# Quantising w_fc in transposed layout, 32-column chunk patterns and one more step of lag in an attention and block-quantised FFN kernel

## The reference, cut to what matters

```python
x = x + attn(layernorm(x));  x = x + ffn(layernorm(x))
# attention: 128 chunk summaries per sequence, each the mean of 64 normalised rows
q = x @ Wq + bq;  k = summary @ Wk + bk;  v = summary @ Wv + bv       # 16 heads of 64
out = softmax(mask(q k^T / 8)) @ v @ Wo + bo
# ffn, 1024 -> 4096 -> 1024
h = gelu(quant(x) @ quant(w_fc).T + b_fc);  y = quant(h) @ quant(w_proj).T + b_proj
def quant(v):   # blocks of 32 along the last dimension
    scale = exp2(floor(log2(max(|block|))) - 3);  return round(v / scale) * scale
```

## Time and profile before

| | us |
|---|---|
| median of three runs | 1062.04 |
| the profiled execution, whole | 1060.65 |
| its span on the slowest core (core 3) | 1059.1 |
| spans of the other cores | 1043.5 to 1057.7 |
| PE, DVE, ACT busy in the span | 759.1, 695.3, 390.2 |

### The profile page before, as it was taken

The page is one execution under the profiler, slowest core; times in us unless marked ns, Lnnn a source line. Parts: engine busy times, 40 slices in busy tenths (PEclk is TensorE's granted clock), DMA queues, the critical chain, the costliest instruction groups (busy, mean ns, idle before and its releaser), DMA issues.

```text
span 1059.1 us, 13616 instructions; the slowest of 8 cores (1043.5 to 1059.1 us)
## 1 busy us (share of the span) xinstructions
PE 759.1 (72%) x4554; PEld 427.1 (40%) x4554; DVE 695.3 (66%) x1039; ACT 390.2 (37%) x623; POOL 114.9 (11%) x171
## 2 busy tenths in 40 slices
PE   0304433635585647769769699999999999999973
PEld 0102111212233212224226475766667675858431
DVE  3557537776733576967557699796969696877601
ACT  2335426565641454425443342323323141505000
POOL 2201213121201000001100000000000000000011
PEclk9997766766877656779889889999999999999987
DMA  8999997899718874743275611232313141302023
GB/s 219 219 198 171 214 232 168 225 212 205 181 66 147 198 199 124 241 146 113 106 219 197 236 34 41 41 60 27 75 20 80 20 81 19 63 6 36 1 40 41
DMA packets 87877, 130.33 MB, mean 123 GB/s; under 512 B 54008, under 2 KB 54144, under 8 KB 85760
## 3 DMA queue, kind: packets, MB, share of 16 engines
q0 software_dynamic: 23312, 57.95, 27.2%
q1 hardware_dynamic: 64496, 71.51, 25.8%
HBM read 112.93 MB, written 25.17 MB: 130 GB/s over the span
## 4 chain that ended last, share of the span: by engine, by line
PE 53%; DMA 16%; DVE 14%; issue 7%; ACT 5%; SPq 3%; DVEq 0%; ACTq 0%; POOL 0%; POOLq 0%
PE psY L1029 11%; PE psX L1029 10%; DMA wst<-wpj_in 6%; PE psS L979 6%; PE psV L979 5%; PE psT L979 4%; PE psO L979 4%; DMA xs<-xoth 4%; SPq L146 3%; DMA wst<-wfc_in 3%; PE psY L614 3%; DMA sel<-sel_in 2%; DVE uq L394 2%; PE psO L792 2%; PE psT L792 2%
## 5 line engine op out<-in xcount | busy, mean ns | idle before, releaser
L1029 PE MATMUL psY<-wpT,hq 128*128 128x512 bf16 x512 | 154.2, 383 | 6.0 <-DVE ob L1044 6.0
L1029 PE MATMUL psX<-wpT,hq 128*128 128x512 bf16 x512 | 153.9, 382 | 0.6 <-DVE ob L1044 0.6
L481 PE MATMUL psX<-lnb,pats 128*128 128x512 bf16 x32 | 15.8, 594 | 171.6 <-ACT lnb L589 171.6
L990 DVE TENSOR_REDUCE hpart<-h 128x256 f32<-128x1024 f32 x56 | 107.6, 1922 | 13.2 <-ACT h L983 13.2
L983 ACT ACTIVATE h<-psV,bfc 128x256 f32<-128x256 f32 x72 | 34.1, 474 | 208.2 <-PE psV L979 205.0
L979 PE MATMUL psS<-xqT,wfcT 128*128 128x256 bf16 x576 | 77.6, 279 | 8.8 <-ACT h L983 8.8
L979 PE MATMUL psV<-xqT,wfcT 128*128 128x256 bf16 x576 | 77.2, 279 | 9.0 <-DMA xqT<-xq 4.7
L614 PE MATMUL psY<-lnT,WA 128*128 128x512 bf16 x256 | 72.5, 444 | 14.4 <-ACT lnT L316 14.4
L361 ACT ACTIVATE uq<-wst 128x2048 bf16<-128x2048 bf16 x32 | 60.9, 1902 | 55.0 <-DMA wst<-wpj_in 36.0
L1012 DVE TENSOR_TENSOR hq<-h,hM 128x1024 bf16<-128x1024 f32 x64 | 78.1, 1220 | 1.0 <-DVE hM L1003 0.2
L1029 PEld LDWEIGHTS psY<-wpT,hq 128*128 128x128 bf16 x512 | 50.4, 98 | 67.9 <-issue 8.6
(11 more groups left out here) (123 smaller groups left out, 1216.6 us busy)
## 6 DMA issues: line engine op xcount, KB each, us to landing
xr<-xown POOLq DMA_DIRECT2D x32, 512.0 KB, 7.1
wst<-wfc_in SPq DMA_DIRECT2D x16, 1024.0 KB, 7.9
wst<-wpj_in SPq DMA_DIRECT2D x16, 1024.0 KB, 8.9
xs<-xoth POOLq DMA_DIRECT2D x24, 512.0 KB, 11.4
wpq_scr<-uq SPq DMA_DIRECT2D x16, 512.0 KB, 7.8
y<-xr POOLq DMA_DIRECT2D x16, 512.0 KB, 3.2
xt<-y SPq DMA_DIRECT2D x16, 512.0 KB, 3.7
wpT<-wpq_scr SPq DMA_DIRECT2D x16, 512.0 KB, 10.1
```

The costliest lines, as they stand in the source:

```text
L990: tr_ = op("vector", lambda E, c=c, dst=dst: E.tensor_reduce(out=dst, in_=h[:, 4 * c:4 * c + 4, :].rearrange("p e t -> p t e"), axis=AXX, ...
L1029: tk = op("tensor", lambda E, e=e, e4=e4, u=u, hf=hf, a=a: E.matmul(f2[a].rearrange("p (c n) -> p c n", n=64), hq[r][:, e4, 128 * u:128 * ...
```

## The change

The changed kernel does the following.

- w_fc arrives from the host already transposed and tiled, [2048, 2048], so that a job's tile has features on partitions and hidden units in the free dimension. It is quantised in place in `wfcT`. The 16 DMA transposes are gone. Since a block of 32 now crosses partitions, three halvings on DVE reduce within a partition (the last writes 256 numbers a partition), 64 KB go to DRAM (`wmx_d`) and come back as `gat`, [128, 4, 256], the same 32 rows copied to four groups of partitions (256 KB). Two more halvings (512 and 256 wide) end the maximum.
- A job now yields 5 times. Its rounding (`weight_round`) is put one job behind its maxima (`weight_max`). `wst` has 3 buffers, and loads are issued three jobs ahead. The stream gives 4 yields a step, attention 1 after each of scores, o_unit and mix.
- Patterns are 32 columns wide, one slot's chunks, with a second pattern for the six tiles that cross into the next slot. One load of 0.57 MB takes the place of four of 0.5 MB. The summary matmuls write 32 partitions of `psX`.
- The stream has one more step of lag: statistics at step k, 1/std and patterns at k+1, matmuls at k+2. There are 4 `xs` buffers and 3 `lnb`. Own tiles go with steps 0 to 15. Drains of queries come one place later in ACT's list. Wq is loaded at the end of step 1, Wv when the last query is done, which is now inside the stream. Three small tables are loaded at the start.
- Values are computed ahead of the row maxima.
- In `o_unit` the residual add on DVE also gives the sum of the row. Two bn_stats (L803) and a bn_aggr (L807) for each tile go, and a Square with accumulation on ACT (`squares`) takes their place, one small DVE operation before it. `squares` is called after `mix`, and in FC1 of the first group right after each `o_unit`.

```diff
@@ weights @@
-        for i in range(8):
-            jobs += [("fc", i), ("pj", i)]
-        jobs += [("pj", i) for i in range(8, 12)]
+        for i in range(4):
+            jobs += [("fc", i), ("pj", 2 * i), ("pj", 2 * i + 1)]
+        for i in range(4, 8):
+            jobs += [("fc", i), ("pj", 4 + i)]
...
+            t = op("vector", lambda E: E.tensor_tensor(
+                out=u[:, 512:768].rearrange("p (g c) -> p g c", g=2), in0=u3[:, :, 0:128],
+                in1=u3[:, :, 128:256], op=ALU.max), after=[t])
...
+            t = dma("sync", f"gw{g}", wmx_d[i].rearrange("p (c n) -> c p n", c=4), u[:, 512:768], after=[t])
+            yield
+            job[n, "max"] = dma("sync", f"gat{g}", gat[g].rearrange("p c n -> p (c n)"),
+                                wmx_d[i].unsqueeze(0).broadcast_to([4, 32, 1024]),
+                                after=[t, gat_free[g]] + (st["gat"] if g == 3 else []))
@@ weight_round @@
+                t = tree(gat[g].rearrange("p (z c) n -> p z (c n)", z=1), 512, t)
+                t = tree(gat[g].rearrange("p (z c) n -> p z (c n)", z=1), 256, t)
...
-            if n + 2 < len(jobs):
-                load_job(n + 2)
+            if n + 3 < len(jobs):
+                load_job(n + 3)
...
-                t = Q.dma_turn(f"uq{b}", wfcT[:, 2 * i:2 * i + 2].rearrange("p t j c -> p (t j) c"), uq[b],
-                               after=[t] + late)
@@ the generator @@
+            for n in range(len(jobs)):
...
+                yield from weight_max(n)
+                if n + 1 < len(jobs) and eligible(n + 1):
+                    weight_abs(n + 1)
+                if due is not None:
+                    yield from weight_round(due)
+                due = n
@@ the stream @@
-        for k in range(NSTEP + 1):
-            if k >= 1:
+        for k in range(NSTEP + 2):
+            if 1 <= k <= NSTEP:
                 rstd(k - 1)
-                scale_patterns(k - 1)
             if k < NSTEP:
                 other_stats(k)
...
+            background(1 if k < NSTEP else 0)
+            queries()
+            if 1 <= k <= NSTEP:
+                rstd_exp(k - 1)
+                scale_patterns(k - 1)
+            if k - 2 in own_tile:
+                pend = own_mm(k - 2)
+            background(1 if k < NSTEP else 0)
...
             if k - 1 in own_tile:
-                pend = own_apply(k - 1)
-            background(3)
-            queries(1)
-            if k >= 1:
-                add_others(k - 1)
+                own_apply(k - 1)
+            if k >= 2:
+                add_others(k - 2)
                 if k + 2 < NSTEP:
                     load_other(k + 2)
+            background(2 if k < NSTEP else 0)
...
+            if k > 17 and not q_todo and t_wv is None:
+                t_wv = dma("gpsimd", "WA", WA, wv_in.rearrange("(j p) n -> p j n", p=128), after=lnT_free)
@@ o_unit @@
-            ts = op("vector", lambda E: E.bn_stats(out=bn2[:, 6 * hf:6 * hf + 6], in_=xx),
-                    after=[tx, bn2_free["tok"]])
@@ squares @@
+                tq = op("scalar", lambda E, t=t, k=k: E.activation(
+                    out=junk2[t // 8], in_=xr[k], func=ACT.Square, bias=nm2[:, t:t + 1], accum_out=ssq[:, t:t + 1]),
+                    after=[ta, sq_prev["tok"], sel_free[0] if t > 7 else None] + xr_free[2])
```

More of the change, by code:

```diff
@@ L358, in weight_abs @@
         def weight_abs(n):
[L359 removed]
+            kind, i = jobs[n]
+            k, t = wload[n]
             hi = wst[k].bitcast(BF16)[:, 1::2]
[L361 to L380 removed]
+            if kind == "fc":
+                u = wfcT[:, 2 * i:2 * i + 2].rearrange("p t j c -> p (t j c)")
+                free = st["stream_end"] if i >= 8 else []
+            else:
+                b = n_pj["i"] % 2
+                n_pj["i"] += 1
+                u, free = uq[b], uq_free[b]
+                job[n, "b"] = b
@@ new lines, in weight_round @@
+        def weight_round(n):
+            kind, i = jobs[n]
+            u = job[n, "u"]
+            t = job[n, "max"]
+            k = wload[n][0]
+            mm = trm[n % 2]
+            if kind == "fc":
+                g = job[n, "g"]
+                G, E8, Bk = 2, 8, 128
+                pw = gat[g][:, 0]
+                t = tree(gat[g].rearrange("p (z c) n -> p z (c n)", z=1), 512, t)
+                t = tree(gat[g].rearrange("p (z c) n -> p z (c n)", z=1), 256, t)
+            else:
+                G, E8, Bk = 1, 32, 64
+                pw = u[:, 0:64]
+                mm = mm[:, 0:64]
@@ L412, in weights @@
         def weights():
-            for n, (kind, i) in enumerate(jobs):
-                while kind == "fc" and i >= 8 and not st["stream_end"]:
-                    yield
-                yield from weight_job(n)
+            weight_abs(0)
+            due = None
+            for n in range(len(jobs)):
+                if (n, "abs") not in job:
+                    if due is not None:
+                        yield from weight_round(due)
+                        due = None
+                    while not eligible(n):
+                        yield
+                    weight_abs(n)
+                yield from weight_max(n)
+                if n + 1 < len(jobs) and eligible(n + 1):
+                    weight_abs(n + 1)
+                if due is not None:
+                    yield from weight_round(due)
+                due = n
@@ L686, in build_nc @@
         t_k = kv_tok[1]
+        tv = None
+        for half in range(2):
+            for j in range(8):
+                op("tensor", lambda E, j=j, half=half: E.matmul(
+                    psX[:, 512 * half:512 * half + 512], summT[:, j, :], WA[:, j, 512 * half:512 * half + 512],
+                    start=(j == 0), stop=False), after=[t_wv, t_smT, t_sm], sig=False)
+            tv = op("tensor", lambda E, half=half: E.matmul(
+                psX[:, 512 * half:512 * half + 512], orow, brow[:, 512 * half:512 * half + 512],
+                start=False, stop=True), after=[t_bv, t_ones])
+        t_v = op("scalar", lambda E: E.activation(out=vv, in_=psX, func=ACT.Identity), after=[tv])
+        t_wa = tv
+        t_bo = dma("gpsimd", "brow", brow, bo_in, after=[tv])
         t_wo = dma("gpsimd", "WB", WB, wo_in.rearrange("(j p) n -> p j n", p=128), after=[tk])
-        background(4)
+        background(2)
         def load_sel(s):
```

399 lines of the change are left out of this document (213 added, 186 removed).

## The result

Over 20 runs of each on the same chips the changed kernel takes 1068.53 us in the median and the kernel before 1062.12. The ratio of after to before is 1.0057 (95% interval 1.004 to 1.0073). The forecast was 994, the range 955 to 1045, and slower had 0.06. It was wrong in sign and by 75 us.

The account below looks back on a forecast made before the run. PE bounds FFN and attention's slots 2 and 3; DMA throughput or latency the stream. Stream -42, turn -11, attention -20, FC1 +5 make -68 from 1059.1, 991.1; adjusted from span to median, 994 us, range 955 to 1045.

Parts of the forecast that it names:

- The gather itself has five yields: Weight jobs in the stream: store and gather, 2 x 5 us, fit in 13 us, so DVE would not wait.
- rival 4: Stream: DVE waits for store and gather, 32 us where 13 are given; +152 us, 1146 us in all; chance 0.05.
- The milder form: Stream: DVE waits less for store and gather, ending between 1146 and the forecast 994; no time or chance of its own.
- SP's wait for the store: SP's queue: wait for the 64 KB store to land before issuing the gather, 5 us, bounds 3 and 9.6.
- The opening: Stream before step 6: fewer bytes and less blocking by transposes bring step 6's start from 96.5 to 86 us.
- The steps: Stream steps 6 to 21: bounded at once by DMA and PE, both near 9.5 us; 10.4 us a step.
- The end of the stream: From the last statistics to the last summary matmul: 8 us, with the stream ending at 267 us.
- The turn: From the stream's last summary matmul to attention's first exp: 34 to 35 us against 46; gain 11, bounds 3 and 14.
- Attention: Attention slots: 35, 54, 48 and 33 us; gains 15 and 12, loss 7; net gain 20, bounds 0 and 30.
- FC1: FC1 of the first group: ACT leaves the gelus for add, small operation and Square; 5 us lost, bounds 0 and 9.
- DMA bytes bound the stream: Stream: 59 MB at 198 GB/s take 298 us, gain 11 in place of 42; 1025 us in all; chance 0.2.
- The waits only change places: SP's store wait is 8 us or more, weight loads late; stream -15, turn -3; 1050 us in all; chance 0.1.

Follow-up runs that it names:

- e1: Changed kernel without the round trip: no store of the maxima, no gather, last two halvings on the job's own tile (other quantisation); 1023.11 us, ratio 0.9611.
- e9: Changed kernel with Wv asked for after the stream's last step, as in the kernel before, in place of step 21; 1070.4 us, ratio 1.0061.
- e8: Changed kernel with SP asking for the gather later, after the next weight load; 1069.59 us, ratio 1.0069.
- e4: Kernel before with each DMA transpose of w_fc replaced by an ordinary copy of the same 512 KB (wrong weights); 1050.84 us, ratio 0.9874.
- e11: The kernel of e10 with three pieces of a weight job per pair in attention's slot 0 in place of two; 1024.81 us, ratio 0.9649.
- e6b: Second run of e6, unchanged, as the measure for the next kernel on the same chip; 1031.86 us, ratio 0.97.
- e10: The kernel of e6 with each Square in FC1 of the first group two products later in ACT's list; 1023.62 us, ratio 0.9625.
- e7: Kernel before without the w_fc transposes and without copies; DVE's subtraction writes wfcT itself (wrong weights); 1044.38 us, ratio 0.9844.
- e6: Changed kernel with one hop for two: six copies within SBUF replace the DRAM store and gather; 1030.87 us, ratio 0.971.

## Where the prediction failed, step by step

**The step that failed: "The gather itself has five yields, 13 us, to store and come back (2 x 5 us): hidden."** The round trip was put at nothing on DVE's path. DVE stood for it 40 to 52 us, and e1 prices it: 45 us over the whole kernel. Both numbers of the sentence were off. The pair was put at 10 us; on core 7 the six pairs of the stream for which DVE stood took 13.3 to 23.4 us from the store's issue to the start of the halvings. And the room for it was put at 13 us; taking DVE's wait from the pair's time leaves 8 to 11 us in five of the six. The pair issued at 64.1 took the longest, 23.4 us, past the 21.5 from which rival 4 decides, and DVE stood 2.4 us for it; that at 279.5 took 20.9, and DVE stood 12.5. This is rival 4's mechanism, "the gather takes the path". Its sum, 1146, let all eight take 32. The milder form between it and the forecast is what came, and I gave it no chance and no time of its own. That is why "slower" had 0.06. The mark named for it, a wait of DVE for `gat` of over 8 us, is in the trace with 12.5.

**Under it: SP's wait for the store.** "I take 5 us, nearer the lower end because of its size." Measured: median 8.1, 2.5 to 3 us where little else moves, up to 15.8. The bound above of 9.6 was too low, since it was a median landing. Size was the wrong guide: how full the engines are with POOL's loads decides most of it (2.6 against 12.5 us above, and e9), and what SP asked for just before adds to it (the 14.8 at 157). The same passage held a second error: the time was compared with nothing. Before, SP was blocked 77 us, and eight waits of 8 to 10 are as much again, so SP was not unblocked at all. e8, in which SP waits some 25 us less and the time is the same, gives no sign that this by itself cost much, though its gather starts later.

**The opening.** 86 forecast, 102.2 measured (before 96.5; e1 92):

```profile
102.19 1.29 DVE L575 BATCH_NORM_STATS2 bnh<-xs 128x6 f32<-128x512 bf16 x2
```

10 of the 16 us missing go with the round trip: DVE stood 9.35 us for the first pair, which was over before Wq was asked for at 50.3, and 2.4 us for the one beside Wq. The later Wq that I named as a risk is not enough by itself: e1 asks for it at the same step and has 92. The other 6 e1 doesn't win either: the gain that I gave for bytes and for the transposes' blocking was too large without it, too.

**The steps.** Steps 6 to 23 take (284.1 - 102.2) / 17 = 10.7 us on this core (10.5 in the median over cores, 10.2 in e1); forecast 10.4 for most of them, before 11.7. POOL's wait under 20 us: 17.6. The lag did what it was to do. But the size of the step is right by luck, since one of its two bounds was not there. PE was put at 7.3 us for two query products, 16 x 0.458, and 9.5 in all. The mean of 458 ns is that of matmuls that overlap; their busy time in the same row is 62.6 us for 210, 0.30 us each, so 4.8 us. PE is busy for 108 of the 182 us of these steps at a clock of 0.78 (6.4 us a step), with the clock at the level that I named as the risk. Nor did DMA bytes bound them at the rate of before: e4 moves as much in its stream as before, 61.3 MB, at 206 GB/s. What bounds a step of 10.2 us in e1 was not shown.

**The end of the stream.** 8 us forecast, 24.7 measured, 12 in e1. Before it had been 12 to 13 too, so the 8 was 4 too short without any round trip. A single late round trip is at its dearest here, as no step is left to absorb it.

**The turn.** 35 forecast, 47 measured, 39 in e1 on its slowest core and 38 in the median. The working held without the round trip; with it the same wait comes once more on DVE, ahead of the negated maxima that PE awaits before the first exp at 356:

```profile
349.50 0.82 DVE L394 TENSOR_TENSOR gat<-gat 128x512 bf16<-128x512 bf16 x2 [9.15 <-DMA gat<-wmx_scr]
...
354.20 0.58 PE L328 MATMUL psT<-ident,nmpad 128*128 128x128 bf16 x4 [12.79 <-DVE nmpad L844]
```

**Attention.** Gain 20 forecast. Slots were 43, 67, 47 and 35 us in after, 43, 60, 47 and 35 in e1, for 35, 54, 48 and 33; the sum of the two light ones was right. Even e1 takes 185 us from the first exp to the end of slot 3, before 190. Two terms were left out. From the last pair of slot 0 to the first of slot 1 pass about 9 us, in before as in e1, and 10 to 15 at the two other crossings; 8 x 4.3 held seven gaps and no crossing. And in slot 0 the pairs of after that carry a |w| follow each other at 5.3 to 5.6 us, those without at 4.35. This is ACT of e1 in order of time:

```profile
336.59 1.01 ACT L945 ACTIVATE eT<-psY 32x1024 bf16<-32x1024 f32 x1 [0.68 <-PE psY L939]
337.51 1.89 ACT L391 ACTIVATE uq<-wst 128x2048 bf16<-128x2048 bf16 x1
```

The exp of the next pair stands behind that |w|. I had counted DVE alone. The lower bound, "0 (the jobs only move)", is near what was measured, and e11 moves them once more for nothing.

**FC1.** 5 us forecast within 0 to 9. The FFN takes 516 us in after and 518 in e1, for 514 before, so 2 to 4. The waits named, of ACT before the Square and of PE for the gelus, are the ones seen, and e6b to e10 puts 8 us on where the Squares stand. Why more can be won there than had been lost was not tried.

**The rivals.** "DMA bytes bound the stream": the 198 GB/s of before are no ceiling. e4 moves 61.3 MB to the end of its stream, as before (61.2), at 206 GB/s with a share of 0.82 for 0.91, and the 59.6 MB of after, 301 us at 198 GB/s, take 309. Fewer bytes may still be a part of what the steps gained: 34.9 MB pass in steps 6 to 23 of after, 39.5 in those of before. Its counterargument "that packets are slow where queues cross" is weak too: the median 4 KB packet of SP's takes 159 ns alone and 172 beside POOL's. "The waits only change places" had the right sentence for SP's queue, but at 1050 the wrong sign, since its price was put at a smaller gain of the stream, 15 us for 42, and not at the trip itself.

**In sum,** by the slowest cores' windows of before, forecast and e1: stream 309, 267 and 279; turn 46, 35 and 39; attention 190, 170 and 185; FFN 514, 519 and 518. So even without the round trip the gain was 38 where 68 were forecast: 12 are missing in the stream (6 in the opening, 4 at the end, the rest in the steps), 4 in the turn and 15 in attention. The round trip takes 45 more, and the gain is gone.

**Open.** The 21 to 25 us from e7 to e1 are lag, buffers, 32-column patterns, fewer bytes and the early Wv together; they weren't parted. ACT's 35.5 us of waiting for a buffer of `pj` in after are under 20 in the kernels without a round trip (19.1 in e6), with nothing changed there, so I read them as a consequence, untested. Why the first slot's PE clock stays at 0.50 in both kernels was not tried.

## What to carry to other kernels

A small transfer that somebody waits for costs what the DMA engines and its own queue are doing at that moment, not what its size says (64 KB took 2.5 to 15.8 us here): price it by the worst landing in the same stretch, look for the large loads of the other queues that will stand beside it, and set the result against the room that the consumer really has. When an expensive operation is replaced, price the waits of the new path against what the old one blocked before counting its removal as a gain; here 16 us were taken out and 45 put in. Where data must cross partitions in a small piece, one hop inside SBUF did in this kernel what a store and a load back did, in 37 us less.

## What the hardware showed that I had not expected

POOL's scaling of a pattern is on average slower with 32 columns (961 ns) than with 128 (701 ns), but its width is not why. These are its shortest, median and longest times in ns, after and before:

```profile
L640 POOL TENSOR_SCALAR psc<-pats,rsa x48: 352/548/2488, 45.8 to 306.2; 128x32 bf16<-128x32 bf16 x48
```

```profile
L570 POOL TENSOR_SCALAR psc<-pats,rsa x48: 592/595/2596, 32.6 to 303.9; 128x128 bf16<-128x128 bf16 x48
```

With nothing on DVE it takes 352 to 363 ns, for 592 to 621. The long ones stand beside an addition, subtraction or maximum of a weight job on DVE, and end 0.1 to 0.2 us after one of these does (the line of POOL holds two, of 2.29 and 1.86 us):

```profile
173.33 2.29 DVE L455 TENSOR_TENSOR uq<-wst,trm 128x2048 bf16<-128x2048 f32 x1
173.56 4.14 POOL L640 TENSOR_SCALAR psc<-pats,rsa 128x32 bf16<-128x32 bf16 x2 [11.96 <-DVE nbo L628]
175.72 1.23 DVE L460 TENSOR_TENSOR uq<-uq,trm 128x2048 bf16<-128x2048 bf16 x1
```

In before most scalings stood beside the statistics of others, or beside nothing, and took 0.59 to 0.62 us; the three beside a job's addition or subtraction that are over 1.3 us there show the same. The new order of the step put the scalings among the pieces of the jobs. So "takes something off POOL" was wrong through what runs beside it: POOL is busy for 77 us of 309 in place of 64.8. What it cost the stream was not tried; POOL waits most of the time.
